# Mixture-of-experts stage: three first-product blocks in flight on three PSUM banks, the second product four blocks behind

## The reference

```
x = x + tanh(g_xattn) * attention_block(layernorm(x), ctx)   # cross, self attention, GELU layer
x = x + tanh(g_ffn)   * moe(layernorm(x))

def moe(x):                       # 8 experts, each token goes to its best 2
    h = rms_weight * x * rsqrt(mean(x*x) + 1e-6)
    top_w, top_i = top_k(softmax(h @ gate_w.T), 2); top_w /= sum(top_w)
    a = h @ w1[e].T               # 256 -> 896
    g = h @ w3[e].T               # 256 -> 896
    eo = (silu(a) * g) @ w2[e].T  # 896 -> 256
    return x + sum over the token's two experts of eo * top_w
```

## Time and profile before

| What | Value |
|---|---|
| median of three runs | 2243.79 us |
| profiled execution: own time, span | 2244.22 us, 2242.5 us |
| granted TensorE clock, whole span | 0.912 |
| PE, DVE, ACT, POOL busy, whole span | 84%, 68%, 53%, 54% |
| PE busy in each 100 us from 1600 to 2200 | 93.3 to 93.8 us |
| POOL busy in the same stretches | 77.1 to 79.1 us |
| DVE, ACT busy in the same | 63.6 to 64.5, 63.3 to 64.8 us |
| granted clock in the same | 1.00 |

### The profile page before, as it was taken

How to read it: one execution, slowest core, us unless ns; L and a number is a source line. 1 busy time by engine, 2 the same in 40 slices (tenths; PEclk the granted TensorE clock), 3 DMA queues, 4 the chain that set the end, 5 groups by cost and what they waited for, 6 DMA issues and landing times. The chain is left out here.

```text
span 2242.5 us, 36497 instructions
## 1 busy us (share of the span) xinstructions
PE 1886.7 (84%) x12326; PEld 1358.7 (61%) x12326; DVE 1515.0 (68%) x3086; ACT 1195.5 (53%) x2271; POOL 1217.5 (54%) x1009
## 2 busy tenths in 40 slices
PE   1897999999999999979947878741999999999996
PEld 0544445555555455535426767640988998998996
DVE  5486678787777777857714888872666666666663
ACT  0165566666666666646624323311666666666663
POOL 6443454645445654432342355541677777777775
PEclk8598899999999999989868889965999999999998
DMA  2555445455565344555011121214666666666662
GB/s 82 126 102 108 107 93 116 91 117 116 111 129 119 90 105 100 100 108 100 16 66 47 44 80 50 83 57 145 201 201 203 185 199 200 190 196 201 193 185 65
DMA packets 117006, 270.75 MB, mean 121 GB/s; under 512 B 15674, under 2 KB 49722, under 8 KB 116436
## 3 DMA queue, kind: packets, MB, share of 16 engines
q1 hardware_dynamic: 102516, 249.70, 41.2%
q0 software_dynamic: 14304, 18.72, 4.6%
HBM read 196.63 MB, written 71.73 MB: 120 GB/s over the span
## 5 line engine op out<-in xcount | busy, mean ns | idle before, releaser
L701 DVE TENSOR_REDUCE nraw<-ps 128x1 f32<-128x512 f32 x1024 | 648.8, 680 | 253.5 <-PE ps L848 252.1
L614 ACT ACTIVATE spare<-ps 128x512 f32<-128x512 f32 x1024 | 571.0, 602 | 386.4 <-PE ps L858 384.6
L1728 POOL TENSOR_TENSOR u_lo<-u_f,u_hi 128x256 fp32r<-128x256 f32 x273 | 342.2, 1263 | 167.0 <-ACT u_hi L1758 167.0
L1829 PE MATMUL ps_e<-x_hi,we_hi 128*128 128x256 f32 x1092 | 316.7, 290 | 4.5 <-DVE we_lo L1650 4.4
L848 PE MATMUL ps<-kst,qst 50*128 50x512 f32 x1024 | 289.3, 458 | 22.3 <-DVE nraw L701 17.0
L1829 PE MATMUL ps_e<-x_hi,we_lo 128*128 128x256 f32 x1092 | 305.6, 280 | 0.0
L1829 PE MATMUL ps_e<-x_lo,we_hi 128*128 128x256 f32 x1092 | 305.5, 280 | 0.0
L870 PE MATMUL ps<-spare,vaug 128*32 128x512 f32 x2048 | 286.6, 633 | 0.0
L858 PEld LDWEIGHTS ps<-qst,kst 52*128 52x128 f32 x1024 | 105.9, 189 | 297.8 <-ACT spare L614 205.3
L858 PE MATMUL ps<-qst,kst 52*128 52x512 f32 x1024 | 280.0, 513 | 7.3 <-ACT spare L614 7.0
L1689 DVE TENSOR_TENSOR u_f<-ps_e,silu 128x256 f32<-128x256 f32 x273 | 115.3, 422 | 237.2 <-PE ps_e L1829 139.0
(11 more groups left out here) (222 smaller groups left out, 3884.0 us busy)
## 6 DMA issues: line engine op xcount, KB each, us to landing
we_raw<-in_experts_w SPq DMA_DIRECT2D x117, 896.0 KB, 4.7
parts_kept<-parts SPq DMA_DIRECT2D x64, 512.0 KB, 3.2
kst<-parts_kept SPq DMA_DIRECT2D x192, 128.0 KB, 4.7
qst<-parts_kept SPq DMA_DIRECT2D x192, 128.0 KB, 6.7
x_raw<-xs SPq DMA_DIRECT2D x39, 259.0 KB, 2.8
x<-sum_tok SPq DMA_DIRECT2D x16, 512.0 KB, 2.6
x_tok<-x SPq DMA_DIRECT2D x16, 512.0 KB, 3.6
x_tok<-in_x SPq DMA_DIRECT2D x8, 512.0 KB, 4.4
```

Of the source, the lines that this page charges most:

```text
L614: act.activation(probs[:, e % 8], ps[:, score_bank(e, par)], ACT.Exp, scale=SCALE).then_inc(exp_made, 1)
L701: dve.tensor_reduce(nraw[:, g % 2, qt, half, i:i + 1], ps[:, max_bank(m, par)], AX.X, ALU.max, negate=True).then_inc(max_made, 1)
L1728: pool.tensor_tensor(u_lo[:, it], u_f[:, slot], u_hi[:, it].bitcast(F32), ALU.subtract).then_inc(ulo_made, 1)
L1829: ins = pe.matmul(ps[:, 2 * slot + c, 0:GR], left, right, start=m == 0, stop=m == len(terms) - 1)
```

## The change

- The two halves of an `up` block lie in one bank (columns 0 to 255 and 256 to 511). Three such banks are used in turn (`UPS` = 3, block count q modulo 3). `up` of block q waits for `u_f` of block q-3. `silu` and `u_f` have three buffers.
- `silu` waits for both halves of the block (`up_mm` of 2q+2) and no longer for the first alone.
- `down` is always four blocks behind (`LAG` = 4). PE's list becomes u0 d3' t0 u1 d4' t1 u2 d5' u3 d6' u4 d0 u5 d1 u6 d2.
- The accumulators have two pairs of banks (3, 4 and 5, 6), used by even and odd steps. `eo` has two buffers.
- Both transposed halves fit in bank 7 side by side, turned at blocks 0 and 1; ACT's `hi_of_x` stand at blocks 1 and 3 and wait for both; DVE's two `lo_of_x` stand at block 4.
- `put_out` of step n-1 moves from ACT's block 2 to block 5. The adds of step n-1 move: the first to POOL's block 5, the second to block 1 of step n+1. Behind the last step stand three adds instead of two.

The core of the diff:

```diff
+UPS, LAG = 3, 4
 # VectorE
-                    dve.wait_ge(silu_made, n * KI + it + 1)
-                    dve.wait_ge(up_mm, n * (2 * KI) + 2 * it + 2)
-                    if positive(n * KI + it - 1):
-                        dve.wait_ge(ulo_made, n * KI + it - 1)
-                    dve.tensor_tensor(u_f[:, slot], ps[:, 2 * slot + 1, 0:GR], silu[:, slot],
+                    q = n * KI + it
+                    dve.wait_ge(silu_made, q + 1)
+                    dve.wait_ge(up_mm, 2 * q + 2)
+                    if q >= UPS:
+                        dve.wait_ge(ulo_made, q - UPS + 1)
+                    dve.tensor_tensor(u_f[:, q % UPS], ps[:, q % UPS, GR:2 * GR], silu[:, q % UPS],
-                    if it in (4, 6):
-                        lo_of_x(n + 1, 1 - k, (it - 4) // 2)
+                    if it == 4:
+                        for mt in range(KD):
+                            lo_of_x(n + 1, 1 - k, mt)
 # GpSimd
-                    if n and it in (3, 6):
-                        add(n - 1, it // 6)
+                    if n >= 2 and it == 1:
+                        add(n - 2, 1)
+                    if n and it == 5:
+                        add(n - 1, 0)
 # ScalarE
-                    act.wait_ge(up_mm, n * (2 * KI) + 2 * it + 1)
+                    act.wait_ge(up_mm, 2 * q + 2)
-                    if it == 2 and n:
+                    if it == 5 and n:
                         put_out(n - 1, 1 - k)
-                    if it in (3, 6) and not last:
-                        hi_of_x(n + 1, 1 - k, it // 6)
+                    if it in (1, 3) and not last:
+                        hi_of_x(n + 1, 1 - k, it // 2)
 # TensorE
                     up(n, k, it)
-                    if it >= 3:
-                        down(n, k, it - 3)
-                    elif it < 2 and not (isinstance(n, int) and n == 0):
-                        down(n - 1, 1 - k, KI - 2 + it)
-                    if it in (2, 5) and not last:
-                        turn_rows(i + k, n + 1, 1 - k, it // 5)
-                down(n, k, KI - 3)
+                    q = n * KI + it - LAG
+                    if q >= 0:
+                        down(q // KI, q // KI % 2, q % KI)
+                    if it < KD and not last:
+                        turn_rows(i + k, n + 1, 1 - k, it)
             over_steps(pe, body)
-            for it in (KI - 2, KI - 1):
+            for it in range(KI - LAG, KI):
                 down(STEPS - 1, (STEPS - 1) % 2, it)
```

More of the change, by code:

```diff
@@ L1595, in expert_phase @@
     x_lo = sb("x_lo", [P, 2, KD, GR], F32R)
-    silu = sb("silu", [P, 2, GR])
-    u_f = sb("u_f", [P, 2, GR])
+    silu = sb("silu", [P, UPS, GR])
+    u_f = sb("u_f", [P, UPS, GR])
     u_hi = sb("u_hi", [P, KI, GR], F32R)
     u_lo = sb("u_lo", [P, KI, GR], F32R)
-    eo = sb("eo_sb", [P, GT, D])
+    eo = sb("eo_sb", [P, 2, GT, D])
     x_in = [sem("x_in0"), sem("x_in1")]
@@ L1616, in expert_phase @@
     added = sem("added")
+    OUT_BANK, X_BANK = UPS, 7
     def over_steps(eng, body, prologue=None):
@@ L1653, in lo_of_x @@
             def lo_of_x(n, k, mt):
-                dve.wait_ge(xhi_made, n * 2 + mt + 1)
-                dve.tensor_tensor(x_lo[:, k, mt], ps[:, 7, 0:GR], x_hi[:, k, mt].bitcast(F32),
+                dve.wait_ge(xhi_made, n * 2 + 2)
+                dve.tensor_tensor(x_lo[:, k, mt], ps[:, X_BANK, mt * GR:(mt + 1) * GR], x_hi[:, k, mt].bitcast(F32),
                                   ALU.subtract).then_inc(xlo_made, 1)
@@ L1718, in add @@
                 pool.indirect_dma_start(
-                    out=scratch["out"], in_=eo[:, t], in_offset=None,
+                    out=scratch["out"], in_=eo[:, n % 2, t], in_offset=None,
                     out_offset=bass.IndirectOffsetOnAxis(ap=targets[:, n % 3, t:t + 1], axis=0),
@@ L1725, in body @@
                 for it in range(KI):
-                    slot = (k + it) % 2
-                    pool.wait_ge(uhi_made, n * KI + it + 1)
-                    pool.tensor_tensor(u_lo[:, it], u_f[:, slot], u_hi[:, it].bitcast(F32),
+                    q = n * KI + it
+                    pool.wait_ge(uhi_made, q + 1)
+                    pool.tensor_tensor(u_lo[:, it], u_f[:, q % UPS], u_hi[:, it].bitcast(F32),
                                        ALU.subtract).then_inc(ulo_made, 1)
@@ L1731, in body @@
                         keep_rows(i, n, k)
-                    if n and it in (3, 6):
-                        add(n - 1, it // 6)
+                    if n >= 2 and it == 1:
+                        add(n - 2, 1)
+                    if n and it == 5:
+                        add(n - 1, 0)
             over_steps(pool, body)
+            add(STEPS - 2, 1)
             for t in range(GT):
@@ L1750, in hi_of_x @@
             def hi_of_x(n, k, mt):
-                act.wait_ge(xt_mm, n * 2 + mt + 1)
-                act.activation(x_hi[:, k, mt], ps[:, 7, 0:GR], ACT.Copy).then_inc(xhi_made, 1)
+                act.wait_ge(xt_mm, n * 2 + 2)
+                act.activation(x_hi[:, k, mt], ps[:, X_BANK, mt * GR:(mt + 1) * GR], ACT.Copy).then_inc(xhi_made, 1)
             def hi_of_u(n, k, it):
@@ L1757, in hi_of_u @@
                     act.wait_ge(down_kt, n * KI + it + 1 - KI)
-                act.activation(u_hi[:, it], u_f[:, (k + it) % 2], ACT.Copy).then_inc(uhi_made, 1)
+                act.activation(u_hi[:, it], u_f[:, (n * KI + it) % UPS], ACT.Copy) \
+                    .then_inc(uhi_made, 1)
             def tanh_of(n):
@@ L1769, in put_out @@
                 act.wait_ge(share_made, n + 1)
-                if n:
-                    act.wait_ge(added, 16 * GT * n)
+                if n >= 2:
+                    act.wait_ge(added, 16 * GT * (n - 1))
                 for t in range(GT):
-                    act.activation(eo[:, t], ps[:, 4 + t, 0:D], ACT.Copy,
+                    act.activation(eo[:, k, t], ps[:, OUT_BANK + GT * k + t, 0:D], ACT.Copy,
                                    scale=shares[:, k, t:t + 1]).then_inc(eo_made, 1)
@@ L1783, in body @@
                 for it in range(KI):
-                    slot = (k + it) % 2
-                    act.wait_ge(up_mm, n * (2 * KI) + 2 * it + 1)
-                    if positive(n * KI + it - 1):
-                        act.wait_ge(u_made, n * KI + it - 1)
-                    act.activation(silu[:, slot], ps[:, 2 * slot, 0:GR], ACT.Silu) \
+                    q = n * KI + it
+                    act.wait_ge(up_mm, 2 * q + 2)
+                    if q >= UPS:
+                        act.wait_ge(u_made, q - UPS + 1)
+                    act.activation(silu[:, q % UPS], ps[:, q % UPS, 0:GR], ACT.Silu) \
                         .then_inc(silu_made, 1)
@@ L1817, in up @@
             def up(n, k, it):
-                slot = (k + it) % 2
-                if positive(n * KI + it - 1):
-                    pe.wait_ge(u_made, n * KI + it - 1)
+                q = n * KI + it
+                if q >= UPS:
+                    pe.wait_ge(u_made, q - UPS + 1)
                 for c in range(2):
@@ L1828, in up @@
                     for m, (left, right) in enumerate(terms):
-                        ins = pe.matmul(ps[:, 2 * slot + c, 0:GR], left, right, start=m == 0,
+                        ins = pe.matmul(ps[:, q % UPS, c * GR:(c + 1) * GR], left, right, start=m == 0,
                                         stop=m == len(terms) - 1)
@@ L1835, in down @@
                     pe.wait_ge(wlo_made, n * 3 + 3)
-                    if positive(n):
-                        pe.wait_ge(eo_made, GT * n)
+                    if n >= 2:
+                        pe.wait_ge(eo_made, GT * (n - 1))
                 pe.wait_ge(ulo_made, n * KI + it + 1)
@@ L1844, in down @@
                     for m, (left, right) in enumerate(terms):
-                        ins = pe.matmul(ps[:, 4 + t, 0:D], left, right, start=it == 0 and m == 0,
+                        ins = pe.matmul(ps[:, OUT_BANK + GT * k + t, 0:D], left, right, start=it == 0 and m == 0,
                                         stop=it == KI - 1 and m == len(terms) - 1)
```

7 lines of the change are left out of this document (3 added, 4 removed).

## The result

The changed kernel took 2181.55 us in the median of four runs (2180.92 to 2188.55), the kernel before 2244.18 in its four; the ratio is 0.972 (0.970 to 0.975). In a second set of runs on one chip it was 0.970 (0.967 to 0.972). Forecast: 2178, range 2166 to 2205.

A forecast was written before the change was run, and what follows sets the result against it. PE was taken as the bound, with 1.82 us of waits in a 16.86 us step. The stage's 590.2 us and the tail gave 2176.9 us, plus 1 us for the first steps: forecast 2178 us, range 2166 to 2205.

The forecast's parts named there:

- The wait at d4: PE waits there once a step for POOL's u_lo, held out by DVE's lo_of_w; 1.24 us, to go.
- A step without waits: Expert phase: 126 matmuls at 0.1159 us and two turns of 0.22 us make 15.04 us, against 16.86.
- 0.1162 us a matmul: Start to start on PE in the new stage, taken a little slower than the mean of 0.1159.
- The three stretches: Parts of one old PE step read as free of waits: 12.52 us for 108 matmuls, 0.1159 us each.
- The placement: New step laid out engine by engine: all five PE waits go, least room for u_lo 2.5 us, at block 2.
- Stage: Expert phase, first to last matmul: 590.2 us, so the last matmul starts at 2155.1, 70.8 us earlier.
- Tail: After the last u6: three chained adds 4.47 us apart, end 23.3 us behind it; gives back 3.5 us.
- POOL at 88% of a step: POOL's busy share of the new expert step, even with its busy time of 13.29 us unchanged.
- DMA share 0.75: DMA engines' busy share in the denser expert step, up from 0.67, not full.
- Landings of adds: POOL's adds each wait for the landing before: median 3.9 us, round trip 4.47 us, kept in the forecast.
- Rival C: POOL's chain of adds: denser transfers double the round trip to about 8.6 us, step 17.2, total 2257 us; chance 4%.
- Rival B: The order doesn't bring it: another wait of 1 to 2 us takes the place, 2230 to 2244 us; chance 4%.

The follow-up runs named there:

- wlo6: The kernel before with DVE's third lo_of_w moved from block 5 to the end of block 6; 2264.48 us, ratio 1.007.
- two halves: The changed kernel with LAG = 2 and each lo_of_w cut into two instructions of 896 columns; 2240.69 us, ratio 0.998.
- dmasmall: The changed kernel with weight loads of 256 of 1792 columns from step 1 on, products wrong; 2188.04 us from one execution.
- after_again: The changed kernel itself, unmodified, run again beside the kernel with the last step reordered; 2179.77 us, ratio 0.970.

## Why the prediction was right, step by step

- **The wait at d4 and its cause.** Right, and shown: the exclusion of `lo_of_w` and `u_lo` sets it (wlo6, two halves), and room between `up` and `down` hides it (LAG 2, 3, 4). One reading was wrong: between its own `up` and d4 stand two `up`, three `down` and a turn, not two `up` and one `down`. It is still one `up` less than d0 to d3 have, and the argument holds. (The add at 1664.24 has 1.57 us in its row, not 1.56.)
- **A step without waits: 15.04, taken as 15.1.** Measured 15.11.
- **0.1162 us a matmul.** The value held (0.1163 in the trace, waits and turns left out), the reason did not: I raised 0.1159 for denser transfers, but dmasmall shows the same 0.1163 with a seventh of each load, and the kernel before has 0.1163 too, outside its waits. The three stretches I read were a little fast. That the value came out is luck in this small part (0.0003 x 4913 = 1.5 us).
- **The placement.** Room of 2.5 us at block 2, measured 2.64; 2.9 at block 0, measured 2.94. DVE, ACT and POOL did what their lists said.
- **Stage.** Last matmul 590.2 us behind the first, measured 593.1. Of the 2.9, 1.5 is the last `down`'s wait for `u_lo` 6 and the slow start behind it. I had seen this wait and left it out of the stage since the adds hide it, which they did. 0.5 lies in the first step, within the 1 us allowed for it (its first 19 starts took 5.22 us and not 4.78; the granted clock was 0.50 and 0.90 in the first two stretches of 5 us, and 0.52 and 1.00 in the kernel before), and 0.9 in the steps behind: 15.10 us each, where 126 x 0.1162 + 0.44 gives 15.08.
- **Tail.** Three adds 4.5 us apart, and an end 23.3 us behind the last u6: they stand 4.4, 4.5 and 4.6 apart, and u6 ends at 2156.4, 23.4 before the end. From there on the tail is as forecast.
- **The 3.6 us by which the span (2179.8) missed 2176.2** (2175.2 and the 1 us for the first steps): 3.2 stand ahead of the stage, where nothing was changed; the stage has 1.9 more, and the stretch behind it 1.5 less, since the late last `down` took its wait out of it. In the traces of kernels with the same code there, the first `up` starts between 1560.2 and 1575.2:

```profile
1562.50 1.12 PE L1821 MATMUL ps_e<-ident,x_raw 128*128 128x128 f32 x4 [44.80 <-DMA x_raw<-xs]
1568.10 0.55 PE L1837 MATMUL ps_e<-x_hi,we_hi 128*128 128x256 f32 x1 [4.48 <-DVE we_lo L1653]
```

- **Wrong in size:** POOL at 88% of a step, measured 11.99 of 15.11, 79%: the cast, 1.98 beside a `lo_of_w` before, now follows the blocked `u_lo` and takes 0.18; the seven `u_lo` of a step take 9.87 us in place of 8.86. DMA share 0.75, measured 0.68: my start, 0.67, was that of one busy step, where the 100 us stretches had 0.63 to 0.66. Landings of adds: I assumed them unchanged, and the median rose from 3.9 to 5.4 us, the most to 8.3. Rival C was nearer than I gave it credit for, but with the adds 8.5 and 6.6 us apart in the step it had no effect on PE.
- **Rival B** had the right idea about the kernel before, of a second wait close behind, and wlo6 met it. The change doubles both `eo` and the accumulators and does not meet it; my placement named these two in one line and did not price what they prevent.

## What to carry over

A wait that one engine shows once a period is first a question of order: count for each consumer how much later it starts than its producer ends, before and after. Here the change took 68 us out of the stage and no instruction became faster. Look for the second-latest wait before removing the latest, since moving one line alone made the kernel slower; with one buffer doubled besides, it brought two thirds of the gain. Then trim: one block of distance, one bank and one pair of accumulators turned out to cost at most 6 us each to give up, each alone (two at a time were not tried), and only the distance below three blocks is dear.

## What was not expected of the hardware

- **Matmuls run at two paces, block by block.** In the changed kernel's first trace, in every step from 5 to 33 and with either buffer, `up` of blocks 1, 4 and 6 and the `down` behind each has its starts 113.3 to 113.7 ns apart, the other blocks' 117.7 to 117.9. The traces with two banks, with LAG = 3 (there the pace goes with the `up`, whatever `down` follows) and with small weight loads have the same pattern. But the block does not fix the pace: in after_again, the same kernel, `up` of block 0 changes it from step to step, and steps of 15.04 and 15.18 us alternate. Its third to twelfth start in two steps in a row, 1.02 and 1.06 us:

```profile
1702.42 0.28 PE L1837 MATMUL ps_e<-x_hi,we_lo 128*128 128x256 f32 x1
...
1703.44 0.28 PE L1837 MATMUL ps_e<-x_hi,we_lo 128*128 128x256 f32 x1
...
1717.46 0.28 PE L1837 MATMUL ps_e<-x_hi,we_lo 128*128 128x256 f32 x1
...
1718.52 0.28 PE L1837 MATMUL ps_e<-x_hi,we_lo 128*128 128x256 f32 x1
```

  Where PE waits (before the change, one pair of accumulators) the blocks mix as well. What sets the pace stays open. An estimate of its worth: four of seven blocks 3.9 ns a matmul faster, 4913 x 4/7 x 3.9 ns = 11 us.
- **A wait costs PE a slow start besides:** the second start behind it comes after 0.19 to 0.23 us in place of 0.12. Behind a turn the gap is the same (1706.56 to 1706.76 above), but there the first start came only 0.03 us after the last transpose, so the two make up for each other.
- **Landings of indirect adds grew by 1.5 us in the median** though their bytes are the same. It is the weight loads that they meet: in dmasmall, the same order with a seventh of each load, the landings are those of the kernel before.

```profile
DMA to landing us min/median/max: 3.5/3.8/5.5
```

  Why they meet more of them than in the kernel before, where the loads are as large, was not tried.
